# An attention and mixture-of-experts kernel: another router product, transposes on VectorE, and another order of the queues

## The reference, cut to what matters

```python
x = x + attn(layernorm(x));  x = x + ffn(layernorm(x))
# attn (linear attention, D = 64)
Q, K, V = h @ wq.T, h @ wk.T, h @ wv.T
out = (Q @ (K.T @ V)) * sqrt(3 / D) @ wo.T
# ffn (8 experts: 4 MLPs of width 128, 4 cheap ones; top 2)
scores = sigmoid(h @ Wr)                       # (tokens, 8)
_, idx = top_k(scores + router_bias, 2)
w = scores[idx] / (sum(scores[idx]) + 1e-9);  cw = scatter(w, idx)
routed = sum_e cw[:, e] * ((silu(h @ Wg[e]) * (h @ Wu[e])) @ Wd[e])   # e = 0..3
routed += (cw[:, 4] + cw[:, 6]) * h + cw[:, 7] * relu(h)
shared = causal depthwise conv of 4 taps over the tokens, + conv_b
```

## Time and profile before

| | |
|---|---|
| median of three runs | 891.4 us (890.39 to 892.38) |
| the profiled execution's own time | 890.12 us |
| its span, first to last instruction | 888.3 us |
| TensorE matmul busy / weight loads busy | 849.0 us (96%) / 754.3 us (85%) |
| VectorE / ACT / GpSimd busy | 752.1 (85%) / 643.2 (72%) / 415.6 (47%) |
| mean granted TensorE clock | 0.99 |

### The profile page before, as it was taken

How to read it: one execution, slowest core, us unless ns; L and a number is a source line. 1 busy time by engine, 2 the same in 40 slices (tenths; PEclk the granted TensorE clock), 3 DMA queues, 4 the chain that set the end, 5 groups by cost and what they waited for, 6 DMA issues and landing times.

```text
span 888.3 us, 16852 instructions
## 1 busy us (share of the span) xinstructions
PE 849.0 (96%) x5437; PEld 754.3 (85%) x5437; DVE 752.1 (85%) x2088; ACT 643.2 (72%) x1366; POOL 415.6 (47%) x590
## 2 busy tenths in 40 slices
PE   5878999999999999999999999999999999899997
PEld 4657988999889998889899998889988998788886
DVE  4668989999899988999899998999889987688884
ACT  5585867887777787787688777777867875666653
POOL 3213535554454554565455544545535544443343
PEclk9798999999999999999999999999999999999999
DMA  9111444344354542434443343444424344333334
GB/s 284 61 49 35 132 144 125 99 121 110 119 143 143 143 110 69 132 120 143 143 120 106 93 136 120 143 144 122 118 72 130 108 120 119 94 94 100 113 83 115
DMA packets 79447, 103.86 MB, mean 117 GB/s; under 512 B 6528, under 2 KB 58880, under 8 KB 79360
## 3 DMA queue, kind: packets, MB, share of 16 engines
q1 hardware_dynamic: 74752, 86.02, 30.5%
q0 software_dynamic: 4608, 16.78, 10.0%
HBM read 68.96 MB, written 17.04 MB: 97 GB/s over the span
## 4 chain that ended last, share of the span: by engine, by line
PE 77%; DVE 9%; ACT 4%; issue 4%; POOL 4%; DMA 1%; POOLq 0%; DVEq 0%; ACTq 0%
PE ps_gu L410 11%; PE ps_gu L412 10%; PE ps_gu L411 10%; PE ps_sh L541 6%; PE ps_y L410 5%; PE ps_y L411 5%; PE ps_y L412 5%; PE ps_sh L531 3%; PE ps_y L460 3%; PE ps_sh L484 2%; POOL rstd L1369 1%; PE ps_gram L476 1%; PE ps_gu L564 1%; PE ps_sh L588 1%; PE ps_gram L618 1%
## 5 line engine op out<-in xcount | busy, mean ns | idle before, releaser
L1387 POOL TENSOR_TENSOR gate<-gate,cwb 128x512 f32<-128x512 f32 x128 | 165.7, 1294 | 277.4 <-ACT gate L765 269.3
L410 PE MATMUL ps_gu<-x2T_hi,wgu_hi 128*128 128x512 f32 x512 | 210.7, 411 | 3.6 <-DVE hid L1055 3.6
L412 PE MATMUL ps_gu<-x2T_hi,wgu_lo 128*128 128x512 f32 x512 | 202.0, 394 | 0.0
L411 PE MATMUL ps_gu<-x2T_lo,wgu_hi 128*128 128x512 f32 x512 | 201.4, 393 | 0.0
L410 PE MATMUL ps_y<-wd_hi,hid_hi 128*128 128x256 f32 x512 | 152.3, 297 | 4.2 <-POOL hid_lo L1392 4.2
L1073 DVE SCALAR_TENSOR_TENSOR conv<-x2T,conv_w,conv 128x512 f32<-128x512 f32 x192 | 153.6, 838 | 0.0
L411 PE MATMUL ps_y<-wd_lo,hid_hi 128*128 128x256 f32 x512 | 144.6, 282 | 0.0
L412 PE MATMUL ps_y<-wd_hi,hid_lo 128*128 128x256 f32 x512 | 144.2, 282 | 0.0
L1062 DVE TENSOR_TENSOR hid_lo<-hid,hid_hi 128x512 fp32r<-128x512 f32 x96 | 83.2, 866 | 38.1 <-ACT hid_hi L758 38.1
L412 PEld LDWEIGHTS ps_gu<-x2T_hi,wgu_lo 128*128 128x128 f32 x512 | 96.4, 188 | 22.1
L410 PEld LDWEIGHTS ps_gu<-x2T_hi,wgu_hi 128*128 128x128 f32 x512 | 96.8, 189 | 20.9 <-DVE hid L1055 4.6
(11 more groups left out here) (126 smaller groups left out, 1886.2 us busy)
## 6 DMA issues: line engine op xcount, KB each, us to landing
cwb<-cw_rows SPq DMA_DIRECT2D x128, 256.0 KB, 4.0
xa<-in_x SPq DMA_DIRECT2D x32, 512.0 KB, 7.5
acc<-in_x SPq DMA_DIRECT2D x32, 512.0 KB, 6.7
acc<-x POOLq DMA_DIRECT2D x32, 512.0 KB, 4.6
out<-acc SPq DMA_DIRECT2D x64, 256.0 KB, 2.4
cwb<-in_wg SPq DMA_DIRECT2D x4, 128.0 KB, 4.1
cwb<-in_wu SPq DMA_DIRECT2D x4, 128.0 KB, 3.9
cwb<-in_wd SPq DMA_DIRECT2D x1, 512.0 KB, 4.7
```

The costliest lines, as they stand in the source:

```text
L410: nc.tensor.matmul(dst, a_hi, b_hi, start=start, stop=False, skip_group_check=True)
L411: nc.tensor.matmul(dst, a_hi, b_lo, start=False, stop=False, skip_group_check=True)
L412: return nc.tensor.matmul(dst, a_lo, b_hi, start=False, stop=stop, skip_group_check=True)
L1387: g.tensor_tensor(gate[:, e % 2], gate[:, e % 2], cwb[:, q, e], ALU.mult).then_inc(gatew_ready, 1)
```

## The change

The diff has four parts.

1. The router's stationary operand is now `wr2`, 32 columns wide: the 8 router columns' high half, their low half, and 16 columns of zeros. The high and low halves of the transposed tokens move past it, 512 tokens at a time, in fp32r. The result is transposed, [32 columns, 512 tokens].
2. VectorE turns that in 32 x 32 blocks from PSUM to SBUF (`logits_turn`), GpSimd adds the high and low columns (`logits_sum`), and SyncE moves the four blocks to the four quarters of the partitions with four DMAs (`move_logits`). ACT reads the logits from SBUF. `cw` is also turned in 32 x 32 blocks by VectorE; PE's transposition and ACT's copy of it go, and the store takes four DMAs, of 16 rows of 128 bytes each, in place of one.
3. ACT writes the high half of the transposed tokens first; the full copy `x2T` waits for VectorE's low half of the same bank.
4. The orders change. VectorE, plain step: conv_tap 0 and 1, x2T_low 0, output 0, hidden 0, x2T_low 1, output 1, first part of conv_tap 2, logits_turn, its second part, hid_low 0, hidden 1, [f_low], norm1_stats, hid_low 1, norm1_aggr, xn_low, hidden 2, residual 0 and 1, norm2_stats, hid_low 2, norm2_aggr, route_scores, route_weights with the turn of `cw`, hidden 3, q_low, xnT_low 0 and 1. The two tiny copies of the statistics go. ACT has the score instructions between `acc` and the relu; hid_high 2 is ahead of silu 3. In the drain steps `hid_low` 3 is VectorE's and `last_low` goes.

```diff
+        wr2 = sb("wr2", [P, HC, SQ], F32R)                    # SQ = 32
+        turned = sb("turned", [SQ, P // SQ, TG, SQ])
+        summed = sb("summed", [SQ, P // SQ, TG, NE])
-        cwT = sb("cwT", [EM * TG, P])
+        cwT = sb("cwT", [P, SQ])
...
+            def move_logits(st):
+                sp.wait_ge(sum_ready, st.before("R", 1, 1))
+                if st.later("R", 1):
+                    sp.wait_ge(cw_ready, st.before("R"))
+                for j in range(P // SQ):
+                    sp.dma_start(logits[j * SQ:(j + 1) * SQ, :], summed[:, j].rearrange("p t e -> p (t e)"))\
+                        .then_inc(logits_loaded, 16)
...
-                sp.dma_start(rows.rearrange("a e (t n) -> (a e t) n", t=TG), cwT[:, :]).then_inc(cw_stored, 16)
-                sp.wait_ge(cw_stored, st.before("R", 16, 16))
+                for j in range(P // SQ):
+                    sp.dma_start(rows[:, :, :].rearrange("a e (t n) -> (a e t) n", t=TG)[:, j * SQ:(j + 1) * SQ],
+                                 cwT[j * SQ:j * SQ + EM * TG, :]).then_inc(cw_stored, 16)
+                sp.wait_ge(cw_stored, st.before("R", 64, 64))
...
             def router(st):
-                pe.wait_ge(x2T_ready, st.before("R", HC, HC))
-                for t in range(TG):
-                    for c in range(HC):
-                        last = nc.tensor.matmul(b[:, t * NE:(t + 1) * NE],
-                                                x2T[:, q, c, PAD + t * P:PAD + (t + 1) * P], wr_sb[:, c], ...
+                pe.wait_ge(x2T_ready, st.before("R", HC, 1))
+                pe.wait_ge(x2Thi_ready, st.before("R", HC, HC))
+                for c in range(HC):
+                    nc.tensor.matmul(b, wr2[:, c], x2T_hi[:, q, c], start=(c == 0), stop=False, ...
+                for c in range(HC):
+                    if c == 1:
+                        pe.wait_ge(x2Tlo_ready, st.before("R", HC, HC))
+                    last = nc.tensor.matmul(b, wr2[:, c], x2T_lo[:, q, c], start=False, stop=(c == HC - 1), ...
...
-            def weights_transpose(st):
-            def logits_copy(st):
-            def weights_copy(st):
...
-                copy(x2T[:, q, c, PAD:PAD + GT], ps_sh[c][:, :]).then_inc(x2T_ready, 1)
                 copy(x2T_hi[:, q, c], ps_sh[c][:, :]).then_inc(x2Thi_ready, 1)
+            def x2T_copy(st, c):
+                act.wait_ge(x2Tlo_ready, st.before("R", HC, c + 1))
+                copy(x2T[:, st.slot("R", 2), c, PAD:PAD + GT], ps_sh[c][:, :]).then_inc(x2T_ready, 1)
...
             def score_size(st):
-                act.wait_ge(logits_ready, st.before("R", 2, 2))
+                act.wait_ge(logits_loaded, st.before("R", 64, 64))
+                nc.scalar.activation(size[:, :], logits[:, :], ACT.Abs).then_inc(size_ready, 1)
...
         # ACT's head(): where the score instructions stand
                 q_high(at("Q", 1, NG))
-                logits_copy(r)
-                score_size(r)
-                score_dip(r)
                 xnT_head(3, 0)
                 xnT_head(3, 1)
                 q_high(at("Q", 2, NG))
+                score_size(r)
+                score_dip(r)
                 norm1(at("L", 6, NG))
...
+                v.transpose(cwT[:, :], cw[:, q].rearrange("p e t -> p (e t)")).then_inc(cwT_ready, 1)
+            def logits_turn(st):
+                dve.wait_ge(router_done, st.before("R", 1, 1))
+                v.transpose(turned[:, :, :, :].rearrange("p j t n -> p t j n"),
+                            ps_sh[0][0:SQ, :].rearrange("p (t j n) -> p t j n", t=TG, j=P // SQ))\
+                    .then_inc(turn_ready, 1)
...
+            def logits_sum(st):
+                pool.wait_ge(turn_ready, st.before("R", 1, 1))
+                g.tensor_tensor(summed..., turned[:, :, :, 0:NE]..., turned[:, :, :, NE:2 * NE]..., ALU.add)\
+                    .then_inc(sum_ready, 1)
```

More of the change, by code:

```diff
@@ L508, in xn_transpose @@
                 pe.wait_ge(xn_ready, st.before("A", TG, TG))
[L510 to L512 removed]
+                if st.on("B"):
                     pe.wait_ge(x1_ready, st.before("B", 2, 2 - c))
@@ L865, in f_copy @@
                            [(f1[:, :], ps_gram[:, 0:H]), (f2[0:D, :], ps_gram[0:D, 0:H])], fhi_out)
-            def logits_copy(st):
-                act.wait_ge(router_done, st.before("R", 1, 1))
-                if st.later("R", 1):
-                    act.wait_ge(cw_ready, st.before("R"))
-                copy(logits[:, :], ps_sh[0][:, 0:TG * NE]).then_inc(logits_ready, 1)
-                nc.scalar.activation(size[:, :], ps_sh[0][:, 0:TG * NE], ACT.Abs).then_inc(logits_ready, 1)
             def halo(st):
@@ L1014, in body @@
                     conv_begin(st)
-                if c_on and not st.drain():
-                    silu(st, 3)
-                    hid_high(st, 2)
                 if st.on("L"):
                     norm1(st)
-                if r_on:
-                    weights_copy(st)
                 if st.on("B") and st.drain():
@@ L1060, in hid_low @@
                 dve.wait_ge(hidhi_ready, st.before("C", EM, e + 1))
+                if e == 1 and st.on("L"):
+                    dve.wait_ge(stat1, st.before("L", TG, TG))
+                if e == 2 - st.drain() and st.on("B"):
+                    dve.wait_ge(stat2, st.before("B", TG, TG))
                 k = e % 2
@@ L1287, in body @@
                         x2T_low(st, 1)
+                        hidden(st, 0)
                     dve.wait_ge(halo_ready, st.before("C", 1, 1))
                     conv_tap(st, 0)
-                if st.on("L"):
-                    norm1_stats(st)
+                    conv_tap(st, 1)
                 if r_on and st.later("C", 1):
                     x2T_low(st, 0)
-                if c_on:
-                    conv_tap(st, 1)
+                if y_on:
+                    output(st, 0)
+                if c_on and st.later("C", 1):
+                    hidden(st, 0)
                 if r_on and st.later("C", 1):
@@ L1332, in body @@
                 if c_on:
+                    hid_low(st, 2)
+                if b_on and not drain:
+                    norm2_aggr(st)
+                if r_on:
+                    route_scores(st)
+                    route_weights(st)
+                if c_on:
                     hidden(st, 3)
+                if c_on and drain:
+                    hid_low(st, 3)
                 if st.on("Q"):
@@ L1438, in body @@
                     gate_weight(st, 1)
+                if r_on:
+                    logits_sum(st)
                 if c_on:
```

153 lines of the change are left out of this document (86 added, 67 removed).

## The result

The changed kernel takes 930.1 us (median; 929.0 to 931.5) beside 890.9 us for the kernel before on the same chip (890.0 to 892.4): ratio 1.043, 95% interval 1.041 to 1.046. The forecast was 876, the range 861 to 898. Both the direction and the range were wrong.

The account below looks back on a forecast made before the run. PE was taken to bound the old kernel (96% busy), the loop through VectorE, SyncE and GpSimd the new one. Steady steps -13.4, end -5.6, head +4: -15.0 on 890.1 gives 875.1, median 876; range 861 to 898.

Parts of the forecast that it names:

- 25 steps between the routers of steps 8 and 33: Steady part: 6.25 rounds of four steps, each 101.9 us against 104.04, so -13.4 us.
- the end: Last steps: residual and statistics ahead of routing remove PE's idle time; -5.6 us together.
- the head: First steps: ACT waits for the first logits and the convolution is late for PE; +4 us, between 0 and +8.
- TensorE: PE's router: four fp32r matmuls, 0.92 us, at most 1.3; saves 0.98 us a step, packed plain step 24.13.
- x2T behind the low half ... 0: ScalarE's silu 1 comes 0.75 us later, gate product 1 with it; PE needs it only for gate_up 5; cost 0.
- The loop: Hidden 0 to written weights, SyncE's stores and loads, gate product, next hidden 0: 25.25 us, taken as 25.1; paces plain steps.
- slower than before: Rival: SyncE's four short-row stores lengthen the loop; over 0.55 us extra, four steps pass 104.04; 901 us at 1 us; chance 0.20.
- VectorE alone needs 24.3 to 24.4: VectorE's own work in a plain step, with logits_turn and the turn of cw added: 24.3 to 24.4 us, over PE's 24.13.
- the first rival: VectorE or PE paces, the loop doesn't: four steps of about 100.0 us, total 865; chance 0.28.
- The turn of the logits: VectorE's logits_turn takes 0.63 us, between 0.2 and 1.2; turning cw adds 0.25 with its wait.
- The detour: Logits' turn, sum and four DMAs land some 5.5 us behind the router, half a microsecond of margin for ACT; counted 0.
- The chain step: One step in four: of the chain's own 3.6 us about 1.5 pass, giving 26.6 us.

Follow-up runs that it names:

- e16: e13 with VectorE's low half of q of group 3 ahead of the first routing in the head: 867.1 us, ratio 0.974.
- e9: The changed kernel with only ScalarE's copy of x2T put back ahead of the high half; four stores and head as changed: 902.8 us, ratio 1.014.
- e1: The changed kernel with the four cwb loads reading rows of the input x at the step's head, not the stored weights: 913.9 us, ratio 1.026.
- e2: The changed kernel with one DMA of 128 rows storing the turned weights instead of four of 16 rows: 911.9 us, ratio 1.024.
- e5: e2 with ScalarE copying x2T ahead of its high half, as before the change: 891.9 us, ratio 1.002.
- e11: e10 with GpSimd's gate product 3 ahead of the relu_add, as before the change: 877.2 us, ratio 0.985.
- e13: e11 with VectorE turning the logits ahead of both halves of tap 2 instead of between them: 868.6 us, ratio 0.973.
- e8: e2 with, in the head, GpSimd's logits sum ahead of norm2's factors and ScalarE's norm1 of group 6 ahead of the score: 904.2 us, ratio 1.016.
- e10: The changed kernel with one store, the x2T copy first and the head's order of e8 together: 886.7 us, ratio 0.995.
- e3: The changed kernel with VectorE's order of before: statistics ahead of hidden 0, routing ahead of residual and second statistics: 970.6 us, ratio 1.090.
- e7: e2 with the logits' 32x32 transposition from PSUM replaced by a copy of the same elements: 907.3 us, ratio 1.020.

## Why the prediction was wrong, step by step

**By place.** The 25 steps between the routers of steps 8 and 33 gave +25.3 us for -13.4 forecast, the end +5.4 for -5.6, the head +9.2 for +4.

**TensorE, right in itself.** Three of the four matmuls stand 0.23 us apart; with everything else out of the way the packed plain step is 24.16 (e16) for 24.13 forecast. In the changed kernel the fourth waits for VectorE's second low half, so from the first to the next group's start it is 1.89 us in the plain step shown (296.53 to 298.42), over my bound of 1.3 and over the 1.70 of the old router:

```profile
298.16 0.42 PE L564 MATMUL ps_sh<-x2T_lo,wr 128*32 128x512 f32 x1 [0.77 <-DVE x2T_lo L1208]
```

PE is not the bound in three steps of four there.

**The step that failed: "x2T behind the low half ... 0".** I priced it as silu 1 coming 0.75 us later, with product 1 behind it. It cost 27.3 us of the 39 (e9 against the changed kernel). ScalarE's rows show where: two waits of 1.04 and 1.89 us a plain step, behind which stand the second high half, silu 1 and, in a chain step, the copy of the Gram matrix, for which PE waits:

```profile
348.24 0.60 ACT L767 ACTIVATE x2T<-ps_sh 128x512 f32<-128x512 f32 x1 [0.76 <-DVE x2T_lo L1208]
348.73 0.38 ACT L767 ACTIVATE gram<-ps_gram 128x256 f32<-128x256 f32 x1
349.16 1.55 PE L630 MATMUL ps_gram<-wvT_sb,gram 128*128 128x64 f32 x12 [0.77 <-ACT gram L767]
```

I followed silu 1 alone, to gate_up 5, and left the others out. Not all of the 27.3 is its own: with one store it is 20.0.

**The loop, right in its mechanism and mis-sized.** Forecast 25.25, taken as 25.1; measured 26.33. VectorE's part from hidden 0 to the written cw took 18.65 instead of 17.9, and 0.6 of that are blocks (1.82 + 0.93 + 1.56, less 0.70 and two of 0.69, is 2.2 for 1.6); the stores took 2.75 for 2.45, the load to the product 3.32 for 3.1. Opened (e1, e2) it gives back 16 to 18 us. The four stores were the rival "slower than before", which landed on the right side for another reason: over my 2.45 they cost 0.3 us, under the 0.55 from which it was to decide, and they land no later than the one of the earlier trace rows. The page's median issue-to-landing of the changed kernel:

```profile
cw_rows<-cwT SPq DMA_DIRECT2D x128, 2.0 KB, 1.4
```

The Trainium skill's fixed cost of about 2.0 us ("DMA: Bandwidth & Descriptors", "Anatomy of one DMA — SWDGE (gpsimd) path") is for a DMA that GpSimd issues; I had applied it to SyncE's store, where 1.4 us is measured. Its read-modify-write under 512 bytes ("Specifications") is not seen in the landing either, which is 1.4 us for rows of 128 bytes as it was for rows of 512.

**"VectorE alone needs 24.3 to 24.4", wrong.** With the loop open it is full in a step of 25.8 (e1), and with one store and the copy first plain steps stand at 25.15 (e5) until GpSimd's product 3 and then the turn are moved (e11, e13). I had put the blocks in the loop's sum only; but a held operation takes VectorE's time whoever paces. That is why the first rival's 865 was out of reach, although VectorE came out as the next bound in e1; e16, with some 0.7 us less held time a plain step than e11, reaches 867.

**The turn of the logits, right:** 0.63 forecast, 0.63 to the next start (299.28 to 299.91), and for cw 0.17 where I had 0.25 (its end at 315.46 to the next start, 315.63). **The detour, nearly right:** I counted 0; ScalarE waited for the logits nine times in 32 steps, 12.7 us, 5.4 of it in the head and at most 1.7 at any other place.

**The chain step, wrong:** 26.6 forecast, 29.5 measured, 27.0 to 27.8 with the copy first and one store (27.45 before). Of the chain's own 3.6 us I let 1.5 pass, over plain steps. In the changed kernel the chain step and the one behind it take 55.2 us and two plain ones 52.9, so 2.3 passed; in e5 it is 2.5.

**The head, the sign right and the size at half:** +4 forecast (0 to +8), +9.2 measured, of which the order of ScalarE and GpSimd is 5.2 to 7.7 us (e8, e10). For one thing I had no term: TensorE's granted clock. In the changed kernel PE is idle from 60 to 68 us, and the clock is at its lower level (0.50, 1.2 GHz) from 65 to 77, and at 0.56 and 0.59 in the mean of 84 to 88 and 88 to 92; before the change it was low from some 73 to 80 only. A gate matmul that takes 0.48 in a packed queue takes 0.79 at that level. By these windows PE is busy for some 9 us more at the lower level, so up to some 4 us of the 9.2 may come of it. That is an estimate; PE is not all that is waited for there, and no run isolates it.

**The end, missed for two reasons.** It was +5.4 us for -5.6: 143.2 us behind the router of step 33, where the kernel before has 137.8. The copy and the four stores, for which I counted nothing there, make up 6.1 of it together (137.1 in e5): the copy 4.2 with one store (141.2 in e2), but only 1.2 with four (141.9 in e9), and the stores the rest. The gain of 5.6 then still doesn't appear: with both put right it is 0.7, with the head's order too 1.0 (136.8 in e10). There the first step is 2.4 us shorter (25.01 for 27.39), where I had 3.5; the next three fall by 0.2 in all, where I had 1.2; and behind the last router it is 1.5 us longer. Why was not looked into.

**The sum.** From 930.1: copy -27.3 (e9), stores -10.9 (e5), head -5.2 (e10) is 886.7. A further gain comes from elsewhere: -9.5 by product 3 (e11), -9.3 by the turn's place (e13). The forecast 876 is near what the change reaches when its held copy, four stores, head and product 3 are put right (877.2), and not what it is. That nearness is in part luck: the 25 steps of e11 take 638.9 us for the 638.6 that I forecast, but with plain steps of 24.9 and chain steps of 27.0 instead of 25.1 and 26.6.

## What to carry to other kernels

Price a wait by its queue: list every instruction behind it up to the next point where that engine is idle anyway, and follow each to who waits for it; a wait on ScalarE counted at nothing was 20 to 27 of the 39 us here. Time taken from the engine that paces is worth only the distance to the next one, and the next one's occupancy must include operations held by a third engine, since moving a row to where that engine works gave 0.4 to 0.6 us a plain step at no change in work (e11, e13 with e16's rows). Undo parts in both orders before naming a cause: the single "order" theory fell in e3, where the cost of the held copy lay on top of it. One corner stays untried: the old router in the new order.

## What the runs showed of the hardware

- Where one of VectorE's operations on two SBUF operands and GpSimd's tensor_tensor overlap, the one that comes second is lengthened (tap half 0.70 to 1.82, the logits' sum 0.44 to 2.13). VectorE's operations with one operand in PSUM ran beside a product at their usual 0.68 to 0.70 (the turn at 476.83 in e16). The Trainium skill says of the port pair that the two share that a VectorE instruction with two SBUF inputs contends with a GpSimd instruction that reads SBUF, and one with at most one such input doesn't ("SBUF — State Buffer", "Who interferes with whom"); these rows agree.
- A product that started right at the end of a tap half, as the 32x512 transposition or copy from PSUM began, took 1.82 to 1.83 us instead of 1.30 (the changed kernel, e7); one that was running when the transposition began took 1.31 (e16). Why wasn't settled; it isn't the transposition.
- 32x32 transpositions of a 32x512 fp32 block from PSUM take 0.70 us, as long as a copy of the same block (0.67); those of 128x32 in SBUF 0.21.
- Four DMAs of 16 rows of 128 bytes hold the issuing queue 1.72 us, one of 128 rows 0.58 us; each of either kind lands in 1.4 us.
